# A graph kernel: hops by gathered rows, against hops by a dense matrix of edge counts

## The reference

```python
h = x @ W_in + b_in
deg_inv_sqrt = where(deg > 0, rsqrt(max(deg, 1)), 0)
edge_weight = deg_inv_sqrt[row] * deg_inv_sqrt[col]
acc = cur = h
for _ in range(3):
    cur = segment_sum(cur[col] * edge_weight[:, None], row, num_segments=N)
    acc = acc + cur
out = layernorm(x + (acc / 4) @ W_out + b_out)
```

## Time and profile before

| | |
|---|---|
| median of 3 runs | 8,068.51 us (8,067.49 to 8,073.63) |
| the profiled execution's own time | 8,049.89 us |
| its span | 8,048.0 us |
| mean granted TensorE clock | 0.813 |
| busy: PE, PEld, DVE, ACT, POOL | 5,706.7; 2,024.2; 4,194.6; 680.2; 5,951.3 us |
| GpSimd's busy time: gathers of the convolutions, of the hops, placings | 2,412.1; 2,465.7; 1,016.9 us |
| moved | 346.49 MB, mean 43 GB/s |

### The profile page before, as it was taken

The page is one execution under the profiler, slowest core; times in us unless marked ns, Lnnn a source line. Parts: engine busy times, 40 slices in busy tenths (PEclk is TensorE's granted clock), DMA queues, the critical chain, the costliest instruction groups (busy, mean ns, idle before and its releaser), DMA issues.

```text
span 8048.0 us, 72860 instructions
## 1 busy us (share of the span) xinstructions
PE 5706.7 (71%) x14185; PEld 2024.2 (25%) x14185; DVE 4194.6 (52%) x10640; ACT 680.2 (8%) x1792; POOL 5951.3 (74%) x5938
## 2 busy tenths in 40 slices
PE   5820058888848888757788777777777777777776
PEld 2300024444413433323333321111111111111111
DVE  8930035555524444424444465555555555655556
ACT  3910001111200000010000010000000000000000
POOL 3877777777777777777777757777677777677774
PEclk8965568878865566676666679999999999999998
DMA  5000012222421111141111111111211111211112
GB/s 162 6 6 1 1 34 53 53 53 53 130 52 51 52 52 52 47 137 52 51 52 52 52 38 25 25 25 25 31 25 25 25 25 25 38 25 25 25 25 33
DMA packets 239208, 346.49 MB, mean 43 GB/s; under 512 B 129619, under 2 KB 138878, under 8 KB 238706
## 3 DMA queue, kind: packets, MB, share of 16 engines
q0 software_dynamic: 182992, 245.38, 14.1%
q1 hardware_dynamic: 55712, 96.16, 3.6%
q10 hardware_dynamic: 130, 0.80, 0.0%
HBM read 253.24 MB, written 87.84 MB: 42 GB/s over the span
## 4 chain that ended last, share of the span: by engine, by line
POOL 32%; PE 27%; DMA 17%; issue 16%; DVE 7%; DVEq 1%; POOLq 0%; ACT 0%; SPq 0%
PE psum L862 14%; POOL msg L507 13%; POOL placed_src L491 12%; PE psum L824 11%; DMA msg<-hop_table,stage_idx 10%; POOL msg L518 6%; DMA msg<-msg_table,visit_src 6%; DVE agg_and L1265 1%; DVE sel L1257 1%; PE psum L760 1%; DVE agg_and L1231 1%; DVE sel L1208 1%; PE psum L807 1%; PE psum L746 1%; DVE bufE L1043 0%
## 5 line engine op out<-in xcount | busy, mean ns | idle before, releaser
L824 PE MATMUL psum<-sel,msg 128*128 128x256 f32 x4980 | 2331.5, 581 | 1337.6 <-DMA msg<-msg_table,visit_src 1188.2
L518 POOL DMA_INDIRECT msg<-hop_table,stage_idx x2418 | 2465.7, 1020 | 850.4 <-issue 370.6
L862 PE MATMUL psum<-sel,msg 128*64 128x512 f32 x4836 | 2497.5, 605 | 744.1 <-issue 376.5
L507 POOL DMA_INDIRECT msg<-msg_table,visit_src x2490 | 2412.1, 969 | 758.9 <-issue 614.1
L824 PEld LDWEIGHTS psum<-sel,msg 128*128 128x128 f32 x4980 | 1095.6, 265 | 2489.8 <-issue 1726.5
L1265 DVE TENSOR_TENSOR agg_and<-agg_and,psum 64x512 f32 x1209 | 821.5, 679 | 1336.5 <-PE psum L862 1335.4
L491 POOL DMA_INDIRECT placed_src<-stage_pay,stage_addr x800 | 1016.9, 1271 | 304.6 <-issue 214.3
L1231 DVE TENSOR_TENSOR agg_and<-agg_and,psum 128x256 f32 x1245 | 523.1, 420 | 1348.3 <-PE psum L824 1166.8
L862 PEld LDWEIGHTS psum<-sel,msg 128*64 128x64 f32 x4836 | 476.0, 135 | 2763.5 <-issue 1458.1
L1257 DVE TENSOR_SCALAR sel<-iota,agg_and 128x512 f32<-128x512 f32 x2418 | 1141.3, 511 | 0.1
L1205 DVE SCALAR_TENSOR_TENSOR sel<-iota,agg_and,psum 128x256 f32<-128x256 f32 x830 | 349.9, 477 | 986.3 <-PE psum L760 985.7
(11 more groups left out here) (201 smaller groups left out, 1748.4 us busy)
## 6 DMA issues: line engine op xcount, KB each, us to landing
msg_table<-sel SPq DMA_DIRECT2D x147, 512.0 KB, 3.9
msg<-msg_table,visit_src POOLq DMA_INDIRECT x2490, 2.5
msg<-hop_table,stage_idx POOLq DMA_INDIRECT x2418, 2.5
placed_src<-stage_pay,stage_addr POOLq DMA_INDIRECT x800, 2.6
hop_table<-sel SPq DMA_DIRECT2D x21, 224.0 KB, 2.8
bufE<-inv_sqrt SPq DMA_DIRECT2D x2, 1568.0 KB, 10.0
out<-cur SPq DMA_DIRECT2D x12, 256.0 KB
placed_src<-sel SPq DMA_DIRECT2D x1, 806.0 KB, 7.1
```

The costliest lines, as they stand in the source:

```text
L507: g.indirect_dma_start(out=msg[:, n % MV, :], out_offset=None, in_=msg_table, in_offset=bass.IndirectOffsetOnAxis(ap=visit_src[:, v:v + 1] ...
L518: g.indirect_dma_start(out=msg[:, b, 0:H], out_offset=None, in_=hop_table, in_offset=bass.IndirectOffsetOnAxis(ap=stage_idx[:, b:b + 1], a ...
L824: t.matmul(psum[:, banks[c % len(banks)], at:at + W2], msg[:, n % MV, :], visit_sel[:, n % SV, :], start=v % 2 == 0, stop=v % 2 == 1).then ...
L862: t.matmul(psum[0:H, b // 2 % PB, :], msg[:, b, 0:H], sel[:, b % SB, :], start=b % 2 == 0, stop=b % 2 == 1).then_inc(summed, 1)
```

## The change

The edges' layout by source window now also stays sorted by destination block inside a window, so that each pair of a destination block (128) and a source window (512), a cell of 49 x 13 = 637, owns a run of edges. For each cell a 128x512 matrix of edge counts is built once, in f16, and stored in DRAM (`counts`, 689 slots of 128 x 1 KB: 637 cells, 48 extra blocks that close a period of 2,048 edges, 4 that are thrown away). The layout is cut in 1,418 blocks of at most 128 edges of one cell; a block's count is a matmul of a destination one-hot (128x128, from ScalarE) with a source one-hot (128x512, from VectorE), plus, where the cell goes on, the block before, carried in by a matmul with an identity (or a zero) matrix. ScalarE copies the result from PSUM, SP stores it. 709 blocks are built among the visits of the second convolution and 709 among those of the third. SP reads where to store from a row.

A hop then holds the state in SBUF as three bf16 parts (high, middle, low; ScalarE and VectorE split it) and multiplies: for each window, 49 blocks times [128 x 128] (high and middle) and [128 x 64] (low), with the counts streamed from DRAM in chunks of 7 blocks (896 KB, 4 chunks in a ring). The last window is 128 wide. VectorE folds the three parts in. Nothing is gathered in the hops; `hop_table` and its stores are gone, and so are `keep_slots`, `turn_runs` and the reload of the placed edges.

The plan changes too: VectorE ranks destinations first (`plan_dst`), then sources; `src_before` comes behind the root product on TensorE. `place_src` issues the scatters straight from the address and payload arrays, 696 ahead of the first convolution and 104 after it, followed by 12 indirect loads of tile rows (`load_tiles`), 24 transposes and seven VectorE operations that make the indices of the one-hots. A new pass counts the edges per cell (VectorE: 50 times two comparisons over 16 columns, with 49 and 13 wide outputs; TensorE: 800 small matmuls), and a plan of some 90 small VectorE operations and 70 matmuls (`plan_cells`, `sum_cells`, `spread_rows`) finds cuts, slots and carries.

```diff
+CUTS = (144, 696, EC)
...
+DQ = 4
+DR = 2
+SR = 12
+KR = 4
+HB = 7
+HG = NBLK // HB
+RING = 4
...
+        counts_dram = dram("counts", (128, NSLOT * BW), F16)
...
+        def blocks_built(k, c=0):
+            return NM * (NQ * (k - 1) + c) // (2 * NQ)
...
+            def store_blocks(k):
+                for m in range(blocks_built(k), blocks_built(k + 1)):
+                    sp.wait_ge(block_kept, m + 1)
+                    at = sp.value_load(store_at[0:1, m:m + 1], min_val=0, max_val=(NSLOT - 1) * BW)
+                    sp.dma_start(counts_dram[:, bass.ds(at, BW)], kept[:, m % KR, :]).then_inc(block_stored[m % KR], 16)
...
+                        sp.dma_start(counts_in[:, n % RING, :, 0:cols],
+                                     counts_dram[:, at:at + HB * BW].rearrange("p (b n) -> p b n", n=BW)[:, :, 0:cols]).then_inc(counts_read[n % RING], 16)
...
+            def place_src(first, last):
+                for c in range(first, last):
+                    g.indirect_dma_start(out=placed["src"][0:E, :], out_offset=bass.IndirectOffsetOnAxis(ap=address["src"][:, c:c + 1], axis=0),
+                                         in_=payload["src"][:, c, :], in_offset=None).then_inc(written["src"][c % 2], 16)
...
-                        g.indirect_dma_start(out=msg[:, b, 0:H], out_offset=None, in_=hop_table,
-                                             in_offset=bass.IndirectOffsetOnAxis(ap=stage_idx[:, b:b + 1], axis=0)).then_inc(gathered[b], 16)
-                turn_loop(pool, turn)
...
-            place("src", CUTS[0], CUTS[1])
+            place_src(CUTS[0], CUTS[1])
             for k in range(LAYERS):
                 for s in range(4):
                     pool.wait_ge(table_out[s], 16 * len(range(s, NBLK * (k + 1), 4)))
                 visit(k)
-                if k + 2 < len(CUTS):
-                    place("src", CUTS[k + 1], CUTS[k + 2])
-            for hop in range(HOPS):
-                for m in range(NHB):
-                    pool.wait_ge(hop_out[m], 16 * (hop + 1))
-                gather(hop)
+                if k == 0:
+                    place_src(CUTS[1], CUTS[2])
+                    pool.wait_ge(visit_added, pairs(1))
+                    load_tiles()
...
+                def one_hots(q):
+                    here = range(DQ * q, min(DQ * q + DQ, NM))
+                    if q >= 2:
+                        act.wait_ge(dst_hot_ready, q - 1)
+                    for m in here:
+                        a1 = a.activation(far[:, q % 2, m % DQ, :], iota16[:, 0:128], ACT.Abs, bias=dst_rel[:, m:m + 1], scale=-1.0)
+                    a1.then_inc(far_ready, 1)
+                    act.wait_ge(far_ready, q + 1)
+                    if q >= DR:
+                        act.wait_ge(block_summed, DQ * (q - DR + 1))
+                    n = len(here)
+                    a.activation(dst_hot[:, q % DR, 0:n, :], far[:, q % 2, 0:n, :], ACT.Relu, bias=ones[:, 0:1], scale=-1.0).then_inc(dst_hot_ready, 1)
+                if k == 1:
+                    one_hots(0)
+                for m in range(first, last):
+                    if m % DQ == 0 and m // DQ + 1 < groups:
+                        one_hots(m // DQ + 1)
+                    act.wait_ge(block_carried, m + 1)
+                    if m >= KR:
+                        act.wait_ge(block_stored[m % KR], 16 * (m // KR))
+                    a.copy(kept[:, m % KR, :], psum[:, 4 + m % 3, :]).then_inc(block_kept, 1)
...
+                    a.copy(parts[:, here, 0:H], psum[:, m, 0:HB * H].rearrange("p (b n) -> p b n", n=H)).then_inc(hop_kept, 1)
+                    act.wait_ge(rest_ready, n + 1)
+                    a.copy(parts[:, here, H:2 * H], rest.rearrange("p (b n) -> p b n", n=H)).then_inc(hop_low, 1)
...
+            dst_before()
+            table_blocks(0, xT, NBLK // 3, NBLK)
+            root_product(0, xT)
             src_before()
...
+                def count_block(m):
+                    pe.wait_ge(dst_hot_ready, m // DQ + 1)
+                    pe.wait_ge(src_hot_ready, m + 1)
+                    if m >= 3:
+                        pe.wait_ge(block_kept, m - 2)
+                    t.matmul(psum[:, 4 + m % 3, :], dst_hot[:, m // DQ % DR, m % DQ, :], src_hot[:, m % SR, :],
+                             start=True, stop=False).then_inc(block_summed, 1)
+                    if m % ROUND == 0 or carry[0] is None:
+                        carry[0] = pe.value_load(carry_pack[0:1, m // ROUND:m // ROUND + 1], min_val=0, max_val=2 ** ROUND - 1)
+                    if m == 0:
+                        last = t.matmul(psum[:, 4, :], carry16[:, 0:128], zeros16[:, :], start=False, stop=True)
+                    else:
+                        by = 7 - m % ROUND
+                        column = ((carry[0] << by) if by >= 0 else (carry[0] >> -by)) & 128
+                        pe.wait_ge(block_kept, m)
+                        last = t.matmul(psum[:, 4 + m % 3, :], carry16[:, bass.ds(column, 128)], kept[:, (m - 1) % KR, :], start=False, stop=True)
+                    last.then_inc(block_carried, 1)
...
-                        t.matmul(psum[0:H, b // 2 % PB, :], msg[:, b, 0:H], sel[:, b % SB, :],
-                                 start=b % 2 == 0, stop=b % 2 == 1).then_inc(summed, 1)
-                turn_loop(pe, turn)
...
+                        for j in range(HB):
+                            b = HB * g + j
+                            flags = dict(start=b == 0, stop=b == NBLK - 1)
+                            t.matmul(psum[:, at % 2, 0:cols], parts[:, b, 0:2 * H], counts_in[:, n % RING, j, 0:cols], **flags)
+                            last = t.matmul(psum[0:H, 2 + at % 2, 0:cols], parts[:, b, 2 * H:3 * H], counts_in[:, n % RING, j, 0:cols], **flags)
+                        last.then_inc(counts_used, 1)
...
+                            pe.wait_ge(extra_read[x % XR], 16 * (x // XR + 1))
+                            if x >= 2:
+                                pe.wait_ge(extras_folded, x - 1)
+                            column = pe.value_load(extra_at[0:1, 0, e:e + 1], min_val=0, max_val=(NBLK - 1) * PARTS)
+                            bank = 4 + 2 * (x % 2)
+                            t.matmul(psum[:, bank, :], flat[:, bass.ds(column, 2 * H)], extra_in[:, x % XR, :], start=True, stop=True)
+                            t.matmul(psum[0:H, bank + 1, :], flat[:, bass.ds(column + 2 * H, H)], extra_in[:, x % XR, :],
+                                     start=True, stop=True).then_inc(extras_used, 1)
...
+                    for lo, of, n in ((0, dst_block, NBLK), (NBLK, src_window, NB)):
+                        last = v.tensor_tensor(cell_hot[:, i % 2, :, lo:lo + n], of[:, here].unsqueeze(2).to_broadcast([EP, CU, n]),
+                                               iota16[0:EP, 0:n].unsqueeze(1).to_broadcast([EP, CU, n]), ALU.is_equal)
...
+                def spread_sources(c):
+                    for m in built(k, c):
+                        if m >= SR:
+                            dve.wait_ge(block_summed, m - SR + 1)
+                        v.tensor_scalar(src_hot[:, m % SR, :], iota16[:, :], src_rel[:, m:m + 1], None, ALU.is_equal).then_inc(src_hot_ready, 1)
...
+                    dve.wait_ge(hop_kept, n + 1)
+                    if n:
+                        dve.wait_ge(parts_ready, n)
+                    v.tensor_tensor(rest_of, psum[:, m, 0:HB * H].rearrange("p (b n) -> p b n", n=H), parts[:, here, 0:H], ALU.subtract).then_inc(rest_ready, 1)
+                    dve.wait_ge(hop_low, n + 1)
+                    v.tensor_tensor(parts[:, here, 2 * H:3 * H], rest_of, parts[:, here, H:2 * H], ALU.subtract).then_inc(parts_ready, 1)
...
+            def fold(to, high, low, folded):
+                link(v.tensor_tensor(to, to, low, ALU.add))
+                link(v.tensor_tensor(to, to, high[H:2 * H], ALU.add))
+                v.tensor_tensor(to, to, high[0:H], ALU.add).then_inc(folded, 1)
```

More of the change, by code:

```diff
@@ L340, in pair_column @@
             return ((pack << -by) if by < 0 else (pack >> by)) & (COLS - 128)
-        def turn_loop(engine, turn):
-            for i in range(NIT - 1):
-                turn(i, B)
-            turn(NIT - 1, LAST_B)
         def apart(engine):
@@ new lines, in sum_cells @@
+            def sum_cells():
+                pe.wait_ge(before_ready, 1)
+                for h, (lo, hi) in enumerate(((0, BW), (BW, CELLS_UP))):
+                    t.matmul(psum[0:NF, h, 0:hi - lo], ones[0:NBLK, 0:NF], before[:, 1 + lo:1 + hi], start=True, stop=True)
+                for j in range(2):
+                    for k in range(CK):
+                        at = 128 * k + 1 - j
+                        last = t.matmul(psum[:, 5, CK * j + k:CK * j + k + 1], before[:, at:at + 128], ones[0:NBLK, 0:1], start=True, stop=True)
+                last.then_inc(cells_summed, 1)
@@ L1359, in _ @@
                 link(v.memset(edge_sums, 0.0))
[L1360 removed]
+                split_parts(hop)
+                hop_folds(hop, edge_sums)
```

604 lines of the change are left out of this document (392 added, 212 removed).

## The result

The changed kernel takes **6,551.8 us** (median of 4 runs, 6,550.77 to 6,554.42) where the kernel before takes 8,068.0 beside it: a ratio of 0.8121, with a 95% interval of 0.8107 to 0.8135. The forecast was 6,170 with a range from 5,930 to 6,720. The profiled execution took 6,550.8 us and has a span of 6,549.0.

The account below looks back on a forecast made before the run. GpSimd's chain of descriptor making (placings and gathers) was taken as the bound; 249 - 22 - 101 + 156 + 3 - 2,172 = -1,887 gave a span of 6,161, forecast as 6,170 us, range 5,930 to 6,720.

Parts of the forecast that it names:

- +249 forecast: Ahead of the first gather: 564 placings left at 440 us, tile loads and cell count move it to 1,325 us.
- 100 two-input comparisons (67 us) delay a descriptor as in the earlier trace: Cell count ahead of the first gather: VectorE's comparisons slow GpSimd's descriptors only mildly; 30 us allowed for the count.
- rival 4: GpSimd starved by VectorE's half-precision comparisons among the gathers: +1,744 us, 7,910; half the gathers, 7,040; chance 0.09.
- The second gap: Between second and third convolution: no placings, only statistics and table stores, 107 us in all, -101 us.
- +3: From third convolution to hops: slots' transposes go (-4 us), the split into parts comes (+7).
- +156 forecast: Count building in two convolutions: ScalarE's one-hots and copies with the carry take 6.4 us per four blocks, 1.37 per visit.
- rival 2: TensorE stays at half clock in the build: 1.67 us per visit, +498 us, 6,670; chance 0.13.
- rival 1: The build hides wholly, convolutions staying at 1.27 us per visit: 6,015 us; chance 0.15.
- -2,172 forecast: Hops: gathers go, dense matmuls come, 335 us per hop and 36 between hops, 1,077 us for 3,249.
- at 0.235 us: 84 chunks x 14: Hop matmuls of 512 columns start 0.235 us apart, weight loads hidden: 275 us per hop.
- rival 3: Slower hops, weights loaded in the open: 0.1 us more per matmul, 113 us per hop, +340, 6,510; chance 0.15.
- Rival 5: Slower than before: hop reads of count rows 689 KB apart, at 83 GB/s 1,027 us a hop, 8,246; chance 0.02.

Follow-up runs that it names:

- last kernel above: Changed kernel with two f16 parts, VectorE waiting for TensorE between cell-count groups, destination one-hots by VectorE; 5,738.5 us for 8,051.5 of the kernel before.
- doubled burst: Changed kernel with four more Abs on ScalarE, written to a spare place, ahead of each four blocks' four; 7,134.9 us (kernel before: 8,051.5).
- Grouping alone: Changed kernel with each hop chunk's seven 128-column matmuls first, then its seven 64-column ones; 6,683.4 us (kernel before: 8,797.1).

## Why the prediction was right, and where it was wrong

**Ahead of the first gather, +249 forecast, +292 measured.** 130 placings were out by 442 us; the 132 forecast came near partly by luck, since the 119 beside the one-hots and the 12 us ahead of them make about 127. The rest went at 1.49 but for some 14 us. The step that failed is "100 two-input comparisons (67 us) delay a descriptor as in the earlier trace rows": I allowed 30 us for the new cell count, and one placing alone stood for 59.3, which is 28 of the 44 us missed. The row that I used had two comparisons and then a pause; a gather could slip in. A hundred without a gap leave none. It is rival 4's mechanism, for 59 us instead of two convolutions, and where VectorE pauses after each pair a placing waits just for the pair (1.95 us). The section of the Trainium skill that I cited on it, "GPSIMD Engine Reference", "Key points", is borne out here, by the two-input instructions. I was wrong to hold the present f32 comparisons (L1208) against it: they read one tensor and take 0.32 us for 256 columns, where the f16 ones take 0.26 us for 512.

**Between the convolutions.** -22 forecast for the first gap, -31 measured: a tile load took 1.25 us (12 from 2,578 to 2,593), not 2.34. The second gap is 17 us too short in the forecast. What I left out: with the build, TensorE lags behind GpSimd by up to the 16 slots, so after the last gather there is a queue to work off: the statistics begin 22 us after it, for 6 before. In the last kernel above, where the burst is gone, this gap is 107 us, what I had forecast; with the burst doubled it is 130. The same stands at the end of the third convolution, where the first step of the normalisation comes 28 us after the last gather for 11 before. The step "+3" for that edge should have been +30: 17 for this queue, and 10 more in the stretch behind it, most of them the first preparation of the parts (seven groups of 2 us are 14, and I had 7).

**The build, +156 forecast, +154 measured** (1,144 + 1,128 against 1,061 + 1,057). The sum 2.1 + 2.3 + 1.8 + waits = 6.4 us per four blocks was right in its total and nearly in its parts: 1.28 + 0.72 us of burst, copies of 0.58, returns of 0.75 for the 0.6 that I had, which is what the unnamed waits stood for; the commonest period is 6.40. The doubled burst shows that the burst stands on the chain that sets the pace. The clock was 0.99 (rival 2 falls), rival 1 falls with the period, and the gathers kept 0.97 us (rival 4).

**The hops, -2,172 forecast, -1,859 measured.** The step that failed is "at 0.235 us: 84 chunks x 14". Rows 7 show loads hidden between matmuls of one width; I carried that to a stream that goes 128, 64, 128, 64. It is rival 3's mechanism at its price: 0.1 us more per matmul, +340 forecast for it, +313 in the stretch. The row that I held against rival 3 was read rightly and did not bear on the case. Grouping alone brings the hops to 1,015, near the 1,077 forecast. Two smaller terms missed in opposite directions: the narrow window takes 21 us per hop and not 7, since its loads stand in the open too (7 to 8 us with one width); and an extra block costs 0.66 us and not 1.0, a term that no row of before showed: its two matmuls follow at 0.33 like the others, the register load adds nothing, and 16 us per hop were too many. The gaps between hops were 34 and 37.3 us (36 forecast).

**The reads.** Hidden, as forecast. The rate that I took from the Trainium skill's "DMA: Bandwidth & Descriptors", section "Latency and other measured facts", for the worst row pitch gave 825 us a hop. It is a figure for copies between DRAM tensors; these are reads into SBUF, and measured with them alone as the bound they reach 410 GB/s, about 210 us a hop, also faster than my 315 to 331 GB/s. Rival 5 was nowhere near.

The forecast was 382 us too low. Its range held the time only since rival 3, to which I gave a chance of 0.15, was in it: rival 3 alone gives 6,510, and the 42 us that are left are about what the stretch ahead of the first gather missed.

## What to carry to other kernels

Before you take a matmul spacing from a row, check that in your stream the number of weight columns is the same from one matmul to the next: splitting a value into 2 + 1 parts of 64 costs more than 2 + 2. When a step moves from one engine to another, price both sides, the chain it lengthens and the engine that it disturbs. And after a stage in which a consumer lags, add the time to work off its queue, not only the last transfer.

## What the runs showed of the hardware that was not expected

- TensorE at full clock, 512 columns, new weights for each matmul: 0.218 us from start to start while the width stays at 128 or at 64, 0.328 where it changes each time. Type of the weights (bf16 or f16 beside f16), PSUM bank and reads beside it made no difference.
- 100 two-input comparisons of VectorE, back to back for 58.6 us, kept one indirect DMA of GpSimd from ending for 59 us, in each of eleven kernels. With one wait of VectorE for TensorE after each pair a placing beside them took 1.95 us, and no indirect DMA over 2.9.
- Reads of 896 KB with 7 KB per row run at 410 GB/s (DMA share 1.01), where the table stores of the earlier trace rows reach 300 to 320.
- Some chips pause. On two chips all engines stand still for one to three us, most often 11 to 12 us apart in the first convolution (116 to 126 late gathers, for 5 to 9 elsewhere). With the build 149 to 190 gathers per convolution are late there, but the chain of the build makes 61 to 73 of them late on a chip without pauses too. The hops show none of it (1,389 to 1,394 us wherever they are those of the change). Both kernels take 7 to 9% longer. The cause stays open.
